# Second relative attention: the queries' write goes ahead of the relative values' read, and the queries' read three operations later on ScalarE

## The chip, the cores and the metric

The kernel runs on one core of a Trainium2 chip. The metric is the device time of one execution in microseconds (us). All numbers of one profiled execution are times from the start of its span.

## What is computed

`x` has 64 samples of 128 tokens with 128 features. Four layers add to it in turn: an attention over feature maps, a mixture of experts, an attention with relative positions, a second mixture of experts. The change lies in the third, which computes this (16 heads of 8 features, 77 keys a sample):

```
q = (query @ Wq + bq)                      # query = layernorm(x); k, v come from ctx
scores = einsum('bhqd,bhkd->bhqk', q, k)
rel_k = rel_key_table[ids]                 # ids = clip(q - k) + 128
scores = scores + einsum('bhqd,qkd->bhqk', q, rel_k)
attn = softmax(scores / sqrt(hd))
out = einsum('bhqk,bhkd->bhqd', attn, v)
out = out + einsum('bhqk,qkd->bhqd', attn, rel_value_table[ids])
x = x + tanh(g_xattn[1]) * (out @ Wo + bo)
```

## The kernel before, in words

`relative_attention` (from L1384) works one sample after the other. Each engine has its own program of slots: slot `n` does the scores of sample `n` and later stages of the samples before it. `slots` (L66) runs slots -4 to 67; the order of operations inside a slot is written out by hand for each engine, and engines meet at semaphores only. `p` is the parity of a sample and picks one of two buffers of nearly every tile; `o` is the other parity.

Two things of a sample make a detour through DRAM, because their rows have to be laid out anew over the partitions:

- The queries. TensorE projects them in slot `n-2` (`project`), ScalarE and VectorE write them as a high and a low float16 part (`high_parts` L1681, `low_parts` L1843, tile `a_q_parts`). SyncE writes them to DRAM (`write_queries`, L1485) once VectorE's part is there (`rows_low`). ScalarE's queue issues the read (`read_queries`, L1658) into `a_q_pos`, once the write has landed (`q_out`) and the scores of two samples before have been made. TensorE's `scores` need it (`q_in`).
- The relative part of the output. TensorE makes it in four quarters (`relative`, L1570), ScalarE copies each out of PSUM (`copy_relative`, L1715, tile `a_rel_all`). After the fourth copy SyncE issues eight writes (`write_relative`, L1492), and when all have landed (`r_out`) the read into `a_rel` (`read_relative`, L1498). GpSimd adds it to the mixed values (`add_relative`, L1777).

GpSimd's slot has three steps: `divide` (L1784), `mask_queries` (L1768, two instructions that spread the queries over the heads, tiles `a_q_head_high` and `a_q_head_low`), `add_relative`. In slot `n` the first is for sample `n-3`, the second for `n+1`, the third for `n-2`. TensorE's `scores(n, p, 0)`, the first step of its slot, waits for both instructions of `mask_queries(n)`.

ScalarE's slot before the change begins with these steps, and ends with `exp(n, 3)`:

```
read_queries(n + 1, o)
copy_rows(n - 2)
high_prob(n - 1, o, 2)
copy_relative(n - 1, o, 0)
high_prob(n - 1, o, 3)
```

`copy_rows` (L1722) takes the sums over the values out of PSUM, `high_prob` (L1703) the transposed probabilities. TensorE's `mix_turn` waits for the first, and its `relative(n-1, o, 1)` for `copy_relative(n-1, o, 0)`.

Of the kernel before, what the change touches and what calls it, by code (L numbers as in the profile page):

```python
# [53 lines left out]
def wait(eng, sem, value):  # L54

    if isinstance(value, int) and value <= 0:
        return
    eng.wait_ge(sem, value)  # L58


def inside(n, lo, hi):

    return lo <= n < hi if isinstance(n, int) else True


def slots(eng, first, lo, hi, last, body):  # L66

    for n in range(first, lo):
        body(n, n % 2)
    if hi > lo:  # L70
        with eng.Fori(0, (hi - lo) // 2) as i:
            for r in range(2):
                body(2 * i + (lo + r), (lo + r) % 2)
    for n in range(max(lo, hi), last):
        body(n, n % 2)
# [1308 lines left out]
def relative_attention(nc, B, io, x_all, stats, mean, rstd, xn_shift, ident, gates, ctx_t, tables, q_dram, r_dram):  # L1384
# [6 lines left out]
    with ExitStack() as ctx:  # L1391
# [80 lines left out]
        with nc.Block(name="a1") as block:  # L1472
            @block.sync
            def _(sp):
                for t, src in WEIGHTS:
                    sp.dma_start(t[:, :], io[src]).then_inc(weights_in, 16)
                sp.wait_ge(cleared, 1)
                for p in range(2):
                    sp.dma_start(q_read[p], q_pos[p][:, :, :]).then_inc(q_zeroed, 16)
                sp.wait_ge(q_zeroed, 32)  # L1480

                def write_queries(n, p):
                    if inside(n, 0, B):
                        sp.wait_ge(rows_low, n + 1)
                        sp.dma_start(q_written[p], q_parts[p][:, :, :].rearrange("q a (d h) -> q (a d) h", d=HD)  # L1485
                                     ).then_inc(q_out[p], 16)

                def write_relative(n, p):
                    if inside(n, 0, B):
                        sp.wait_ge(rel_copied, 4 * n + 4)  # L1490
                        for c in range(QC):
                            sp.dma_start(r_written[p][c], rel_all[p][c:P:QC, :, HD * c:HD * (c + 1)]  # L1492
                                         ).then_inc(r_out[p], 16)

                def read_relative(n, p):
                    if inside(n, 0, B):
                        sp.wait_ge(r_out[p], (n - p) * QC * 8 + QC * 16)
                        sp.dma_start(rel[p][:, :, :].rearrange("q h d -> q (h d)"), r_dram[p]).then_inc(r_in[p], 16)  # L1498

                def slot(n, p):  # L1500
                    read_relative(n - 2, p)
                    write_queries(n + 2, p)
                    write_relative(n - 1, 1 - p)

                slots(sp, FIRST, LO, HI, LAST, slot)

            @block.tensor
# [141 lines left out]
            def _(act):  # L1649
# [4 lines left out]
                def read_queries(n, p):  # L1654
                    if inside(n, 0, B):
                        act.wait_ge(q_out[p], (n - p) * 8 + 16)
                        wait(act, score_ready, 4 * n - 4)
                        act.dma_start(q_pos[p][:, :, :], q_read[p]).then_inc(q_in[p], 16)  # L1658
# [7 lines left out]
                def high_parts(n, p):  # L1666
                    o = 1 - p
                    if inside(n, -2, B):
                        act.wait_ge(proj_ready, n + 3)
                        if inside(n + 1, 0, B):  # L1670
                            wait(act, score_ready, 4 * n)
                            last = nc.scalar.activation(k_t[o][0][:, :], prep_ps[:, K_COLS], ACT.Identity,
                                                        bias=b_k[:, 0:1])
                        if inside(n, 0, B):
                            wait(act, mix_ready, n - 1)
                            last = nc.scalar.activation(value[p][:, :, 0:HD],
                                                        prep_ps[0:KC, V_COLS].rearrange("k (h d) -> k h d", d=HD),
                                                        ACT.Copy)
                        if inside(n + 2, 0, B):
                            wait(act, q_out[p], (n + 2 - p) * 8)  # L1680
                            nc.scalar.activation(q_parts[p][:, 0, :], prep_ps[:, ROW_COLS], ACT.Copy)  # L1681
                            wait(act, q_head_ready, 2 * n + 2)
                            last = nc.scalar.activation(q_t[p][0][:, :], prep_ps[:, Q_COLS], ACT.Identity,
                                                        bias=b_q[:, 0:1])
                        last.then_inc(proj_high, 1)

                def normalize(n, p):
                    if inside(n, 0, B):
                        wait(act, xn_t, n - 1)
                        nc.scalar.activation(xn[p][:, :], x_all[:, n, :], ACT.Identity, bias=xn_shift[:, n, :],  # L1690
                                             scale=rstd[:, n, :]).then_inc(xn_ready, 1)

                def exp(n, u):
                    if inside(n, 0, B):
                        act.wait_ge(shifted, 4 * n + u + 1)
                        nc.scalar.activation(prob[u][:, :, :], prob[u][:, :, :], ACT.Exp, scale=SCALE).then_inc(exped, 1)

                def high_prob(n, p, u):
                    if inside(n, 0, B):
                        act.wait_ge(prob_ready, 4 * n + u + 1)  # L1700
                        wait(act, rel_ready, 4 * n + u - 7)
                        wait(act, mix_ready, n - 1)
                        nc.scalar.activation(prob_t[p][0][:, 4 * u:4 * u + 4, :],  # L1703
                                             trans_ps[u % 2][0:KC, :].rearrange("k (g r) -> k g r", g=4),
                                             ACT.Copy).then_inc(prob_high, 1)

                def copy_relative(n, p, u):
                    if inside(n, 0, B):
                        act.wait_ge(rel_ready, 4 * n + u + 1)
                        if u == 0:  # L1710
                            wait(act, r_out[p], (n - p) * QC * 8)
                            wait(act, r_in[p], (n - p) * 8)
                        if u == 3:
                            wait(act, mixed_ready, n - 1)
                        nc.scalar.activation(rel_all[p][:, 4 * u:4 * u + 4, :].rearrange("r g w -> r (g w)"),  # L1715
                                             rel_ps[:, 0:4 * QC * HD], ACT.Copy).then_inc(rel_copied, 1)

                def copy_rows(n):
                    if inside(n, 0, B):
                        act.wait_ge(mix_ready, n + 1)  # L1720
                        wait(act, rows_turned, n)
                        nc.scalar.activation(mixed_rows[:, :, :].rearrange("r u q -> r (u q)"), rows_ps[:, :],  # L1722
                                             ACT.Copy).then_inc(rows_copied, 1)

                def high_mixed(n, p):
                    if inside(n, 0, B):
                        act.wait_ge(mixed_turned, n + 1)
                        wait(act, y_ready, n - 1)
                        nc.scalar.activation(mixed_t[p][0][:, :], fin_ps[:, 0:P], ACT.Copy).then_inc(mixed_high, 1)

                def slot(n, p):
                    o = 1 - p
                    read_queries(n + 1, o)
                    copy_rows(n - 2)
                    high_prob(n - 1, o, 2)
                    copy_relative(n - 1, o, 0)
                    high_prob(n - 1, o, 3)
                    high_parts(n, p)
                    copy_relative(n - 1, o, 1)
                    exp(n, 0)  # L1740
                    exp(n, 1)
                    copy_relative(n - 1, o, 2)
                    high_prob(n, p, 0)
                    normalize(n + 4, p)
                    high_mixed(n - 3, o)
                    exp(n, 2)
                    high_prob(n, p, 1)
                    copy_relative(n - 1, o, 3)
                    copy_xn(n + 3, o)
                    exp(n, 3)  # L1750

                slots(act, FIRST, LO, HI, LAST, slot)

            @block.gpsimd
# [315 lines left out]
```

## Time and profile before

| | us |
|---|---|
| median of 3 runs | 2211.84 (2209.42 to 2215.06) |
| the profiled execution | 2210.14, span 2208.4 |
| TensorE busy | 2051.3 (93%) |
| VectorE busy | 1913.1 (87%) |
| ScalarE busy | 1554.9 (70%) |
| GpSimd busy | 1575.4 (71%) |

Busy time is a sum over four layers with different limits, so these shares do not say what the changed stage is bound by. The second attention runs from about 1211 to 1800 us of the span. There the order of its slots and who waits for whom matter, read from the waits and from the timeline of each engine. The names ending in q (SPq, ACTq) are an engine's queue, which issues DMAs.

### The profile page before, as it was taken

The page shows a single profiled execution, that of the slowest core. Times are in us where ns is not written, and L with a number is a line of the kernel's source. Part 1 is how long each engine was busy: PE and PEld are TensorE (multiplying, and loading weights), DVE is VectorE, ACT ScalarE, POOL GpSimd, SP SyncE. Part 2 cuts the span into 40 slices and gives each one's busy share as a digit, 9 for nine tenths or more (in the row PEclk, how much of TensorE's full clock was granted, in tenths as well). Part 3 has the DMA queues.
Part 4 walks back from the last instruction along what each step waited for, and adds up shares of the span by engine and source line. Part 5 has one row for each costly group of instructions (what it writes and reads, how often), then busy time and mean ns, then how long its engine had stood idle before and what let it go on. Part 6 is the DMA issues. An engine that isn't in the chain of part 4 may idle for free. (4 is left out here: it accounts for less than half of the span.)

```text
span 2208.4 us, 82850 instructions
## 1 busy us (share of the span) xinstructions
PE 2051.3 (93%) x28378; PEld 1570.9 (71%) x28380; DVE 1913.1 (87%) x4327; ACT 1554.9 (70%) x3516; POOL 1575.4 (71%) x1457
## 2 busy tenths in 40 slices
PE   3999999977999999999996899999999966999999
PEld 2788888854666666666664889999999953666666
DVE  5899999987888888888887789999999868888888
ACT  3788888865555555555554677777777756888887
POOL 1567777643666666666665889999999943888887
PEclk9999999988999999999998899999999978999999
DMA  5000000004322222222221445555555520000000
GB/s 155 12 6 6 6 6 6 7 1 90 93 90 80 81 87 80 81 88 78 83 79 26 78 78 86 80 80 85 82 80 80 84 67 1 15 9 14 9 14 15
DMA packets 476443, 121.41 MB, mean 55 GB/s; under 512 B 431879, under 2 KB 446855, under 8 KB 475604
## 3 DMA queue, kind: packets, MB, share of 16 engines
q1 hardware_dynamic: 343988, 86.86, 18.2%
q10 hardware_dynamic: 132384, 33.63, 6.7%
q8 instruction: 42, 0.69, 0.1%
q14 instruction: 29, 0.24, 0.0%
HBM read 106.51 MB, written 13.89 MB: 55 GB/s over the span
## 5 line engine op out<-in xcount | busy, mean ns | idle before, releaser
L1220 POOL TENSOR_TENSOR f_low<-f_hidden,f_high 128x512 f16<-128x512 f32 x336 | 442.6, 1323 | 217.0 <-ACT f_high L1152 215.1
L1178 DVE TENSOR_TENSOR f_hidden<-f_hidden,f_share 128x512 f32<-128x512 f32 x336 | 374.1, 1114 | 0.0
L1367 POOL TENSOR_TENSOR f_low<-f_hidden,f_high 128x512 f16<-128x512 f32 x256 | 297.1, 1161 | 74.5 <-ACT f_high L1310 74.1
L1158 ACT ACTIVATE f_act_out<-f_gate 128x512 f32<-128x512 f32 x336 | 200.4, 597 | 192.4 <-PE f_gate L1122 192.4
L1201 DVE SCALAR_TENSOR_TENSOR f_hidden<-f_up,f_act_out 128x512 f32<-128x512 f32 x336 | 229.7, 684 | 83.6 <-PE f_up L1122 50.6
L1152 ACT ACTIVATE f_high<-f_hidden 128x512 f16<-128x512 f32 x336 | 210.5, 626 | 73.0 <-DVE f_hidden L1178 71.7
L1132 PE MATMUL f_y<-w_high,f_high 128*128 128x128 f16 x1344 | 242.4, 219 | 2.2 <-POOL f_low L1220 2.2
L1132 PE MATMUL f_y<-w_high,f_low 128*128 128x128 f16 x1344 | 242.4, 219 | 0.0
L1132 PE MATMUL f_y<-w_low,f_high 128*128 128x128 f16 x1344 | 242.4, 219 | 0.0
L1768 POOL TENSOR_TENSOR a_q_head_high<-a_q_t_high,a_head_mask 128x2048 f16<-128x2048 f16 x64 | 232.9, 3639 | 8.0 <-DVE a_q_t_low L1845 8.0
L1768 POOL TENSOR_TENSOR a_q_head_low<-a_q_t_low,a_head_mask 128x2048 f16<-128x2048 f16 x64 | 232.9, 3639 | 0.0
L1353 DVE SCALAR_TENSOR_TENSOR f_hidden<-f_in,f_act_out 128x512 f32<-128x512 f32 x256 | 175.6, 686 | 50.6 <-ACT f_act_out L1317 50.6
L1876 DVE TENSOR_TENSOR a_prob_t_low<-a_trans,a_prob_t_high 77x512 f16<-77x512 f32 x256 | 171.0, 669 | 39.6 <-ACT a_prob_t_high L1703 37.7
L1317 ACT ACTIVATE f_act_out<-f_in 128x512 f32<-128x512 f32 x256 | 152.9, 597 | 65.8 <-PE f_in L1279 60.3
L1548 PE MATMUL a_score<-a_k_t_high,a_q_head_high 128*128 128x77 f16 x1024 | 185.3, 203 | 9.6 <-POOL a_q_head_low L1768 6.4
L1291 PE MATMUL f_y<-w_high,f_high 128*128 128x128 f16 x1024 | 184.8, 219 | 1.8 <-DVE x_all L1331 0.6
L1548 PE MATMUL a_score<-a_k_t_low,a_q_head_high 128*128 128x77 f16 x1024 | 184.9, 203 | 0.0
L1550 PE MATMUL a_score<-table_high,a_q_pos 128*128 128x77 f16 x1024 | 184.8, 203 | 0.0
L1550 PE MATMUL a_score<-table_low,a_q_pos 128*128 128x77 f16 x1024 | 184.8, 203 | 0.0
L1548 PE MATMUL a_score<-a_k_t_high,a_q_head_low 128*128 128x77 f16 x1024 | 184.7, 202 | 0.0
L1291 PE MATMUL f_y<-w_high,f_low 128*128 128x128 f16 x1024 | 184.6, 219 | 0.0
L1291 PE MATMUL f_y<-w_low,f_high 128*128 128x128 f16 x1024 | 184.6, 219 | 0.0
(279 smaller groups left out, 8165.1 us busy)
## 6 DMA issues: line engine op xcount, KB each, us to landing
f_share<-expert_shares SPq DMA_DIRECT2D x128, 256.0 KB, 3.2
a_q_pos<-queries ACTq DMA_DIRECT2D x64, 512.0 KB, 4.4
f_share<-expert_shares SPq DMA_DIRECT2D x128, 128.0 KB, 3.0
relative_values<-a_rel_all SPq DMA_DIRECT2D x512, 8.0 KB, 2.5
x_all<-in_x SPq DMA_DIRECT2D x4, 1024.0 KB, 7.8
f_share<-expert_shares SPq DMA_DIRECT2D x128, 32.0 KB, 1.8
queries<-a_q_parts SPq DMA_DIRECT2D x64, 64.0 KB, 3.0
a_rel<-relative_values SPq DMA_DIRECT2D x64, 64.0 KB, 1.7
```

Source lines behind the costliest of these rows:

```text
L1132: mm = nc.tensor.matmul(dst, h[r][:, own], w_down[part][:, m, :], start=(m == 0 and t == 0 and k == 0), stop=(m == M - 1 and k == 2), skip ...
L1152: nc.scalar.activation(high[r][:, :], hidden[r][:, :], ACT.Copy).then_inc(high_ready, 1)
L1158: nc.scalar.activation(act_out[m % RING][:, :], gate_ps[m % BANKS][:, :], ACT.Silu, scale=1.0 / WSCALE).then_inc(act_ready, 1)
L1178: nc.vector.tensor_tensor(hidden[r][:, :], hidden[r][:, :], share[k][:, :, :].rearrange("p t q -> p (t q)"), ALU.mult).then_inc(scaled, 1)
L1201: nc.vector.scalar_tensor_tensor(out=hidden[r][:, :], in0=up_ps[m % BANKS][:, :], scalar=1.0 / WSCALE, in1=act_out[r][:, :], op0=ALU.mult, ...
L1220: nc.gpsimd.tensor_tensor(low[r][:, :], hidden[r][:, :], high[r][:, :], ALU.subtract).then_inc(low_ready, 1)
L1291: mm = nc.tensor.matmul(dst, h[m % RING][:, own], w_down[part][:, m, :], start=(c == 0 and t == 0 and k == 0), stop=(c == per - 1 and k == 2),
L1353: nc.vector.scalar_tensor_tensor(out=dst, in0=src, scalar=scalar, in1=a, op0=op, op1=ALU.mult).then_inc(hidden_ready, 1)
L1367: nc.gpsimd.tensor_tensor(low[k][:, :], hidden[k][:, :], high[k][:, :], ALU.subtract).then_inc(low_ready, 1)
L1548: nc.tensor.matmul(dst, q[:, QC * g:QC * (g + 1), :], t[:, :], start=(k == 0), stop=False)
L1550: mm = nc.tensor.matmul(dst, q_pos[p][:, g, :], key_table[k][:, 0, window], start=False, stop=(k == 1))
L1768: nc.gpsimd.tensor_tensor(q_head[p][k][:, :, :], q_t[p][k][:, :].unsqueeze(2).broadcast_to([P, P, NH]), head_mask[:, :].unsqueeze(1).broad ...
```

## The change

Two steps change places in two slots. On SyncE the write of the queries of sample `n+2` is issued before the read of the relative values of sample `n-2`. On ScalarE the read of the queries comes after `copy_rows`, `high_prob` and `copy_relative`. Nothing is added or removed.

```diff
@@ -1498,8 +1498,8 @@  (SyncE)
                 def slot(n, p):
+                    write_queries(n + 2, p)
                     read_relative(n - 2, p)
-                    write_queries(n + 2, p)
                     write_relative(n - 1, 1 - p)
@@ -1730,10 +1730,10 @@  (ScalarE)
                 def slot(n, p):
                     o = 1 - p
-                    read_queries(n + 1, o)
                     copy_rows(n - 2)
                     high_prob(n - 1, o, 2)
                     copy_relative(n - 1, o, 0)
+                    read_queries(n + 1, o)
                     high_prob(n - 1, o, 3)
                     high_parts(n, p)
                     copy_relative(n - 1, o, 1)
```

SyncE's queue in the middle slots, where two slots make one turn of the loop, before:

```order
L1498 DMA a_rel<-relative_values 128x128
L1484 REGISTER_ALU
L1485 DMA queries<-a_q_parts 128x16x16
L1490 ISA
L1492 DMA relative_values<-a_rel_all 16x16x8 x8
```

and after:

```order
L1485 DMA queries<-a_q_parts 128x16x16
L1497 ISA
L1498 DMA a_rel<-relative_values 128x128
L1490 ISA
L1492 DMA relative_values<-a_rel_all 16x16x8 x8
```

The write of the queries now stands behind the eight writes of the slot before, and the read of the relative values behind it.

ScalarE, from the last operation of one slot to `high_prob(n-1, o, 3)` of the next, before:

```order
L1696 ACTIVATE a_prob<-a_prob 128x308
L1656 REGISTER_ALU
L58 ISA
L1658 DMA a_q_pos<-queries 128x16x128
L1722 ACTIVATE a_mixed_rows<-a_rows 128x512
L58 REGISTER_ALU
L1703 ACTIVATE a_prob_t_high<-a_trans 77x512
L58 REGISTER_ALU
L1715 ACTIVATE a_rel_all<-a_rel 128x256
L58 REGISTER_ALU
L1703 ACTIVATE a_prob_t_high<-a_trans 77x512
```

and after:

```order
L1696 ACTIVATE a_prob<-a_prob 128x308
L1722 ACTIVATE a_mixed_rows<-a_rows 128x512
L58 REGISTER_ALU
L1703 ACTIVATE a_prob_t_high<-a_trans 77x512
L58 REGISTER_ALU
L1715 ACTIVATE a_rel_all<-a_rel 128x256
L1656 REGISTER_ALU
L58 ISA
L1658 DMA a_q_pos<-queries 128x16x128
L58 REGISTER_ALU
L1703 ACTIVATE a_prob_t_high<-a_trans 77x512
```

The DMA and its two waits (L1656, L58) moved behind three ACTIVATEs.

## Rows read from the trace of the kernel before

**Rows 1.** Busy time by stretch: second attention, and its middle; columns in the first line.

```profile
core 0: us, PE busy (x) PEld busy (x) DVE busy (x) ACT busy (x) POOL busy (x), PEclk, DMA share, GB/s
1211.00:1800.00 589.00, 560.55 (x12719) 521.07 (x12719) 509.95 (x1399) 431.72 (x1274) 515.11 (x254) 0.98 0.50 79
1340.00:1740.00 400.00, 391.94 (x9020) 365.44 (x9017) 362.11 (x999) 305.11 (x907) 366.21 (x182) 1.00 0.52 82
```

**Rows 2.** Waits, 1340 to 1740 us: engine, what, releaser: us in total, times, longest.

```profile
ACT a_mixed_rows L1722 <- DMA queries<-a_q_parts: 69.5, 46, 1.9
POOL a_mixed L1777 <- DMA a_rel<-relative_values: 30.3, 45, 1.0
...
PEld a_rel L1570 <- issue: 8.3, 32, 0.4
...
PE a_score L1548 <- POOL a_q_head_low L1768: 3.5, 11, 0.4
```

**Rows 3.** GpSimd's instructions of line L1768, 1340 to 1740 us.

```profile
L1768 POOL TENSOR_TENSOR a_q_head_high<-a_q_t_high,a_head_mask x46: 3635/3640/3645, 1340.0 to 1736.6; 128x2048 f16<-128x2048 f16 x46
```

**Rows 4.** Timeline of GpSimd: start, us, instruction, [idle before and releaser].

```profile
1607.98 3.64 POOL L1768 TENSOR_TENSOR a_q_head_low<-a_q_t_low,a_head_mask 128x2048 f16<-128x2048 f16 x1
1612.23 0.46 POOL L1777 TENSOR_TENSOR a_mixed<-a_mixed,a_rel 128x128 f32<-128x128 f32 x1 [0.61 <-DMA a_rel<-relative_values]
1612.77 0.41 POOL L1784 TENSOR_TENSOR a_mixed<-a_mixed,a_rden 128x128 f32<-128x128 f32 x1
1613.13 3.64 POOL L1768 TENSOR_TENSOR a_q_head_high<-a_q_t_high,a_head_mask 128x2048 f16<-128x2048 f16 x1
1616.73 3.64 POOL L1768 TENSOR_TENSOR a_q_head_low<-a_q_t_low,a_head_mask 128x2048 f16<-128x2048 f16 x1
1621.01 0.46 POOL L1777 TENSOR_TENSOR a_mixed<-a_mixed,a_rel 128x128 f32<-128x128 f32 x1 [0.63 <-DMA a_rel<-relative_values]
```

**Rows 5.** Timeline of TensorE around the first scores of slots, and in one slot.

```profile
1603.04 0.21 PE L1548 MATMUL a_score<-a_k_t_high,a_q_head_high 128*128 128x77 f16 x1
...
1611.95 0.21 PE L1548 MATMUL a_score<-a_k_t_high,a_q_head_high 128*128 128x77 f16 x1 [0.29 <-POOL a_q_head_low L1768]
...
1613.35 0.64 PE L1559 MATMUL a_trans<-a_by_head_ident,a_prob 128*77 128x128 f32 x4
...
1614.37 0.19 PE L1570 MATMUL a_rel<-table_high,a_prob_t_low 77*128 77x64 f16 x1
...
1620.51 0.21 PE L1548 MATMUL a_score<-a_k_t_high,a_q_head_high 128*128 128x77 f16 x1
...
1629.47 0.21 PE L1548 MATMUL a_score<-a_k_t_high,a_q_head_high 128*128 128x77 f16 x1 [0.27 <-POOL a_q_head_low L1768]
```

**Rows 6.** Timeline of SyncE's queue, two slots (a write of eight counts as one row).

```profile
1603.90 5.10 SPq L1492 DMA_DIRECT2D relative_values<-a_rel_all  x8
...
1612.48 5.11 SPq L1492 DMA_DIRECT2D relative_values<-a_rel_all  x8
1619.17 0.34 SPq L1498 DMA_DIRECT2D a_rel<-relative_values  x1
1619.62 0.37 SPq L1485 DMA_DIRECT2D queries<-a_q_parts  x1
```

**Rows 7.** Timeline of ScalarE and its queue over the start of two slots.

```profile
1605.19 0.38 ACTq L1658 DMA_DIRECT2D a_q_pos<-queries  x1
...
1612.08 0.38 ACT L1715 ACTIVATE a_rel_all<-a_rel 128x256 f32<-128x256 f32 x1
...
1613.93 0.39 ACTq L1658 DMA_DIRECT2D a_q_pos<-queries  x1
1614.51 0.60 ACT L1722 ACTIVATE a_mixed_rows<-a_rows 128x512 f32<-128x512 f32 x1 [1.54 <-DMA queries<-a_q_parts]
1615.00 0.58 ACT L1703 ACTIVATE a_prob_t_high<-a_trans 77x512 f16<-77x512 f32 x1
1615.48 0.38 ACT L1715 ACTIVATE a_rel_all<-a_rel 128x256 f32<-128x256 f32 x1
1615.75 0.60 ACT L1703 ACTIVATE a_prob_t_high<-a_trans 77x512 f16<-77x512 f32 x1
```

**Rows 8.** Landing of the fourth of the eight writes issued from 1612.48.

```profile
L1492 SPq DMA_DIRECT2D relative_values<-a_rel_all x1: 612/612/612, 1614.4 to 1614.4; - x1
...
DMA to landing us min/median/max: 3.9/3.9/3.9
```

**Rows 9.** Landing of the first of the eight, and of the eighth.

```profile
L1492 SPq DMA_DIRECT2D relative_values<-a_rel_all x1: 538/538/538, 1612.5 to 1612.5; - x1
...
DMA to landing us min/median/max: 1.9/1.9/1.9
...
L1492 SPq DMA_DIRECT2D relative_values<-a_rel_all x1: 609/609/609, 1617.0 to 1617.0; - x1
...
DMA to landing us min/median/max: 2.2/2.2/2.2
```

**Rows 10.** An early slot: queues of SyncE and ScalarE, GpSimd, landing of the eighth write.

```profile
1294.31 5.11 SPq L1492 DMA_DIRECT2D relative_values<-a_rel_all  x8
1301.61 0.34 SPq L1498 DMA_DIRECT2D a_rel<-relative_values  x1
...
1296.89 0.39 ACTq L1658 DMA_DIRECT2D a_q_pos<-queries  x1
...
1303.45 0.46 POOL L1777 TENSOR_TENSOR a_mixed<-a_mixed,a_rel 128x128 f32<-128x128 f32 x1 [1.55 <-DMA a_rel<-relative_values]
...
DMA to landing us min/median/max: 2.8/2.8/2.8
```

**Rows 11.** VectorE's low part of the queries; DMA issues: KB each, median us to landing.

```profile
1617.75 0.28 DVE L1843 TENSOR_TENSOR a_q_parts<-a_prep,a_q_parts 128x128 f16<-128x128 f32 x1
...
a_q_pos<-queries ACTq DMA_DIRECT2D x64, 512.0 KB, 4.4
...
queries<-a_q_parts SPq DMA_DIRECT2D x64, 64.0 KB, 3.0
a_rel<-relative_values SPq DMA_DIRECT2D x64, 64.0 KB, 1.7
```

## The prediction

> **What bounds the kernel now.** The busy times by stretch come first. In the middle of the second attention TensorE is busy for 391.94 of 400 us, GpSimd for 366.21 and VectorE for 362.11 [rows 1]. That looks like a stage bound by TensorE, but a share says nothing about who sets the pace, so the waits come next. The largest is ScalarE's: 69.5 us in 46 slots before its copy of the mixed rows, 1.5 us a slot, released by the landing of the queries' write [rows 2]. This is the wait that the change goes for. The second is GpSimd's for the relative values, 30.3 us in 45 slots, 0.67 each. TensorE waits for GpSimd's `a_q_head_low` in only 11 [rows 2].
>
> The small waits lead to the pace. GpSimd masks 46 samples between 1340.0 and 1736.6 us [rows 3], so a slot is 396.6 / 45 = 8.81 us. Its own work in one is two masks of 3.64, an add of 0.46 and a divide of 0.41, about 8.15; the rest is its wait for the relative read [rows 4]. Its masks end at 1611.62 and 1620.37 (start plus 3.64, rows 4), and TensorE's first scores of the slots start 0.33 and 0.14 later [rows 5]. So TensorE enters both slots on GpSimd's release, even where the modelled end of its last matmul hides the gap.
>
> Hence the loop, followed over three slots: scores start at 1603.04 [rows 5]; the fourth copy of the relative part ends on ScalarE at 1612.46 (1612.08 plus 0.38, rows 7); SyncE issues its first write at 1612.48, and the read at 1619.17 [rows 6]; GpSimd adds at 1621.01 [rows 4], then has a divide and two masks to do, and scores start at 1629.47 [rows 5]. That is 9.42 + 8.55 + 8.46 = 26.43 us for three slots, 8.81 each: exactly the slot length. **A delay d in this loop costs d / 3 per slot, and a gain in it gives as little.** ScalarE's wait of 1.5 us is not one of its links: it falls at the start of a slot, and TensorE's work lies between it and the fourth copy.
>
> **The change, part by part.** *SyncE.* The queries' write was issued after the relative read, at 1619.62 [rows 6]. It now needs SyncE free (1612.48 + 5.11 = 1617.59, rows 6) and VectorE's low part (1617.75 + 0.28 = 1618.03, rows 11), so it goes out at about 1618.1, 1.5 us earlier. Its 0.37 us of issue end before 1619.17, when the relative read could start, so the read is not held on SyncE: cost nothing, as long as the eight writes land no sooner than that; with that cover gone SyncE would owe the read up to 0.45 us (wait for VectorE) plus 0.37. The write lands 3.0 us after issue [rows 11], at 1621.1, well before its reader needs it.
>
> *ScalarE's wait* goes: from 1.5 us to nothing. What is late next is TensorE. Its transposes start at 1613.35 for 0.64 us and the relative quarter's last matmul at 1614.37 for 0.19 [rows 5]. So ScalarE's `high_prob` can start at about 1614.15, and `copy_relative` 0.48 later (as 1615.00 to 1615.48, rows 7), at 1614.64 instead of 1615.48. The queries' read follows at about 1615.0, 1.1 us later than now (1613.93). ScalarE needs 0.58 from that issue to its next operation (1613.93 to 1614.51, rows 7), so `high_prob(n-1, o, 3)` starts near 1615.6 instead of 1615.75. Of 1.5 us of wait only 0.15 are left there. The gain inside the loop is TensorE's: it stands before `relative` L1570 for 8.3 us in 45 slots [rows 2], 0.18 us each, mostly for the copy that now comes 0.8 us earlier. I take 0.18 as gained. The landing of the queries, 4.4 us after issue [rows 11], moves to 1619.4; scores need it at 1620.51 [rows 5]. Covered by 1.1 us; without that cover each microsecond would be paid in full.
>
> *What the later read collides with.* The eight writes of the relative part are issued over 5.1 us from 1612.48, the queries' read (512 KB) at 1613.93 in their midst. The first write lands after 1.9 us, the fourth, issued 0.5 us behind the read, after 3.9, the eighth after 2.2 [rows 8, 9]: the read holds up the writes issued behind it, and they have just about caught up by the eighth. Only the eighth counts, since the relative read waits for all. With the read at 1615.0, 2.5 us after the first write, the hold falls on the last three or four. One early slot shows this timing: writes from 1294.31, the queries' read at 1296.89, 2.58 us behind. There the eighth landed after 2.8 instead of 2.2 us, the relative read went out 7.30 us after the first write instead of 6.69, and GpSimd's add came 9.14 after it instead of 8.53 [rows 4, 6, 10]. The slot from 1603.90 with its read 1.29 behind had 8.33 [rows 4, 6, 7]. So three points: 1.29, 1.45 and 2.58 us behind give 8.33, 8.53 and 9.14. From the mean of the first two, 8.43, to 2.5 behind I read +0.65, nearest to the third row. Ends: 0 if the writes escape, about +1.95 if the queries' write, which takes 3.0 - 1.7 = 1.3 us longer to land than the relative read [rows 11] and now is ahead of it in the same queue, is waited for in full. I take nothing for the latter: the write goes out a microsecond ahead of the read.
>
> The Trainium skill's page "DMA: Bandwidth & Descriptors", section "Queues, rings and completion order", says that each DMA engine takes turns between the queues it has work for, packet by packet. By that rule the writes would slip in between the packets of the queries' read, the hold would be nothing, and the sum -3.6 instead of +9.4 us. The trace does not agree: 3.9 us for the fourth write.
>
> *Sum.* Per loop of three slots +0.65 - 0.18 = +0.47, per slot +0.157, over some 60 of 64 slots (the first and last run on other waits) +9.4 us. On the profiled execution's 2210.1 us that is 2219.5; the median of the runs lies 1.7 us above it, so 2221.
>
> **The rivals.** *Nothing moves* (22%). The writes' delay is absorbed or does not occur, and the 0.18 us of TensorE are all that comes: -0.18 / 3 x 60 = -3.6, about 2208. For it: the eighth write was issued 2 us behind the late read. Against: the slot from 1294.31 [rows 10]. By the rule of the skill named above this is the outcome.
>
> *Faster* (8%). The later read lets most writes through before it starts, and the tail that still reaches the eighth now (2.2 us against 1.9 for the first, rows 9) is gone: -0.3 - 0.18 per loop, -9.6 us, 2202. It decides if the read's hold starts only after the eighth write is on its way, which needs the read some 4 us behind the first write rather than 2.5. ScalarE would have to reach it much later than its rows allow.
>
> *Much slower* (15%). The relative read also queues behind the queries' write. If a third of the 1.3 us shows, d grows by 0.45: (0.65 + 0.45 - 0.18) / 3 x 60 = +18, 2230; in full +35, 2247. It decides where the write's transfer is not over when the read is issued; for it speaks that held writes push that transfer later, against it that the read is pushed as far.
>
> *TensorE was the bound after all.* Then GpSimd's lateness costs less than a third of d per slot, since its 0.67 us of wait are slack. It gives 2208 to 2214 and is counted with the first rival. Against it stand 0.33 and 0.14 us between masks and scores in both parities.
>
> **How the numbers follow.** My forecast has 55%, and by itself runs from 2215 (d = 0.4) to 2227 (d = 1.0). A measurement of this kernel tells about 0.3% from no change, 6.6 us: slower begins at 2218.5. Slower: four fifths and more of the 55% and the 15%, some 0.61. Same: the 22% and the forecast's low end, less a little that could be faster, 0.30. Faster 0.09. The range, 2206 to 2232, takes in the first rival and the lower part of the much slower one, and leaves out the faster one and the worst.
>
> **What would show it.** Right: ScalarE's wait for `queries<-a_q_parts` gone from the waits; queries' read about 3.1 us after the first scores of a slot and 2.5 after the first of the eight writes; the eighth write landing after 2.7 to 3 us; GpSimd's wait before L1777 risen from 0.67 to above 0.8 a slot; slots of 8.95 us or more. Wrong: the eighth write still at 2.2 us; GpSimd's wait unchanged; or slots that lengthen while masks end well before the scores start, which would mean a wait for `a_q_pos`.

## The result, and the profile after

The changed kernel takes 2233.97 us (median of 4 runs, 2230.78 to 2236.23) against 2212.32 us for the kernel before on the same chip (4 runs, 2209.42 to 2215.06): ratio 1.0097, 95% interval 1.0079 to 1.0115. It is slower by 21.7 us, where 9 were forecast, and it lies 2 us above the range. Its profiled execution took 2233.33 us, with a span of 2231.5.

Nearly all of the loss is in the second attention: from the first start of GpSimd's masks to the last it takes 582.6 us (1215.3 to 1797.9) instead of 561.5 (1211.3 to 1772.8), 21.1 of the 23.1 us by which the two profiled spans differ. The busy times of the middle 400 us of the changed kernel, answering to [rows 1], and the first and last mask there, answering to [rows 3]:

```profile
1340.00:1740.00 400.00, 371.25 (x8638) 351.80 (x8634) 350.04 (x958) 301.10 (x869) 350.14 (x174) 1.00 0.50 79
```

```profile
L1768 POOL TENSOR_TENSOR a_q_head_high<-a_q_t_high,a_head_mask x44: 3636/3642/3646, 1336.4 to 1732.6; 128x2048 f16<-128x2048 f16 x44
```

Every engine does less in the same time, TensorE too (371 us instead of 392), and a slot takes 396.2 / 43 = 9.21 us instead of 8.81. The waits of the changed kernel over the same stretch, to be read against [rows 2]:

```profile
ACT a_prob_t_high L1703 <- PE a_trans L1559: 57.0, 88, 2.8
POOL a_mixed L1777 <- DMA a_rel<-relative_values: 46.3, 42, 2.8
PEld a_score L1548 <- issue: 32.7, 40, 1.9
PE a_score L1548 <- POOL a_q_head_low L1768: 27.8, 37, 1.8
```

ScalarE's wait for the queries' write, 69.5 us before, is gone. Its wait for TensorE's transposes rose instead, from 10.2 to 57.0 us. GpSimd's wait for the relative values rose from 30.3 us in 45 slots to 46.3 in 42, from 0.67 to 1.10 each. TensorE's wait for GpSimd's masks, 3.5 us in 11 slots before, is now 27.8 in 37: it enters its slots on GpSimd's release.

One slot of the changed kernel shows how. First SyncE's queue, to be read against [rows 6]:

```profile
1500.80 5.11 SPq L1492 DMA_DIRECT2D relative_values<-a_rel_all  x8
1506.65 0.37 SPq L1485 DMA_DIRECT2D queries<-a_q_parts  x1
1508.77 0.33 SPq L1498 DMA_DIRECT2D a_rel<-relative_values  x1
```

Then ScalarE and its queue, against [rows 7]:

```profile
1501.16 0.60 ACT L1722 ACTIVATE a_mixed_rows<-a_rows 128x512 f32<-128x512 f32 x1
1502.77 0.59 ACT L1703 ACTIVATE a_prob_t_high<-a_trans 77x512 f16<-77x512 f32 x1 [1.00 <-PE a_trans L1559]
1503.35 0.38 ACT L1715 ACTIVATE a_rel_all<-a_rel 128x256 f32<-128x256 f32 x1
1503.62 0.39 ACTq L1658 DMA_DIRECT2D a_q_pos<-queries  x1
```

GpSimd, against [rows 4]:

```profile
1505.82 3.64 POOL L1768 TENSOR_TENSOR a_q_head_low<-a_q_t_low,a_head_mask 128x2048 f16<-128x2048 f16 x1
1510.63 0.46 POOL L1777 TENSOR_TENSOR a_mixed<-a_mixed,a_rel 128x128 f32<-128x128 f32 x1 [1.17 <-DMA a_rel<-relative_values]
```

And the landing of the eighth write, issued at 1505.3, against [rows 9]:

```profile
L1492 SPq DMA_DIRECT2D relative_values<-a_rel_all x1: 609/609/609, 1505.3 to 1505.3; - x1
...
DMA to landing us min/median/max: 3.5/3.5/3.5
```

The queries' read goes out 2.82 us behind the first write, the eighth write lands after 3.5 us instead of 2.2, the relative read goes out 7.97 us behind the first write instead of 6.69, and the add comes after 9.83 instead of 8.53.

### The profile page after: what moved, and what is told of

Its sections match the earlier page's. It is cut to its first block and busy times, and to the rows that moved or that the text cites. A ratio compares the mean times of both kernels' runs of the same rounds, so it can differ in the third digit from the quotient of the medians.

```text
span 2231.5 us, 82852 instructions
## 1 busy us (share of the span) xinstructions
PE 2051.4 (92%) x28380; PEld 1578.7 (71%) x28380; DVE 1917.8 (86%) x4327; ACT 1566.3 (70%) x3516; POOL 1573.6 (71%) x1457
## 5 line engine op out<-in xcount | busy, mean ns | idle before, releaser
L1768 POOL TENSOR_TENSOR a_q_head_high<-a_q_t_high,a_head_mask 128x2048 f16<-128x2048 f16 x64 | 233.1, 3641 | 8.0 <-DVE a_q_t_low L1845 8.0
L1768 POOL TENSOR_TENSOR a_q_head_low<-a_q_t_low,a_head_mask 128x2048 f16<-128x2048 f16 x64 | 232.9, 3640 | 0.0
L1703 ACT ACTIVATE a_prob_t_high<-a_trans 77x512 f16<-77x512 f32 x256 | 151.0, 590 | 111.9 <-PE a_trans L1559 87.7
```

The costliest lines, as they stand in the source:

```text
L1768: nc.gpsimd.tensor_tensor(q_head[p][k][:, :, :], q_t[p][k][:, :].unsqueeze(2).broadcast_to([P, P, NH]), head_mask[:, :].unsqueeze(1).broad ...
```

## The experiments

Four numbers are compared throughout. They are means over the slots of samples 14 to 55, each taken from the timelines as in the slot above: **slot** is the time from the first scores of one sample to those of the next; **read Q**, **read R** and **add** are the issue of the queries' read, the issue of the relative read and GpSimd's add, all counted from the issue of the first of the eight writes. **R to add** is the difference of the last two. The ratio is against the kernel before on the same chip. The experiments ran on four other chips, where that one takes 2216 to 2217 us, 4 to 5 more than on the first, so times are compared only through ratios. It was profiled on the first chip and on one of the others, the changed kernel on the same two. The two profiles of one kernel differ by up to 0.07 us in the slot and up to 0.18 in the other columns, so smaller differences between rows are not resolved. A ratio of 0.9992 for the kernel before against itself shows what a ratio can be off.

| | ratio (95%) | slot | read Q | read R | R to add | add |
|---|---|---|---|---|---|---|
| before, first chip | 1 | 8.81 | 1.46 | 6.70 | 1.84 | 8.54 |
| before again | 0.9992 (0.9982 to 1.0002) | 8.88 | 1.54 | 6.84 | 1.88 | 8.72 |
| changed, first chip | 1.0097 (1.0079 to 1.0115) | 9.22 | 2.86 | 7.83 | 1.98 | 9.82 |
| changed again | 1.0086 (1.0068 to 1.0104) | 9.24 | 2.87 | 8.01 | 1.92 | 9.93 |
| SyncE's exchange alone | 1.0013 (1.0004 to 1.0022) | 8.95 | 0.00 | 6.55 | 2.60 | 9.16 |
| ScalarE's move alone | 1.0044 (1.0031 to 1.0057) | 9.11 | 2.76 | 7.67 | 1.94 | 9.61 |
| exchange, read after 1 operation | 1.0019 (1.0008 to 1.0029) | 8.95 | 0.01 | 6.56 | 2.59 | 9.14 |
| exchange, read after 2 operations | 1.0036 (1.0021 to 1.0052) | 9.04 | 2.07 | 7.27 | 2.08 | 9.36 |
| exchange, half a queries' write | 0.9941 (0.9918 to 0.9963) | 8.74 | -0.28 | 6.49 | 1.97 | 8.46 |
| two writes on ScalarE | 1.0066 (1.0052 to 1.0081) | 9.28 | 1.84 | 6.66 | 1.90 | 8.55 |
| one write on ScalarE, read late | 1.0020 (1.0010 to 1.0030) | 9.03 | 2.67 | 7.48 | 1.89 | 9.38 |
| two writes, read late | 0.9985 (0.9975 to 0.9994) | 8.92 | 2.58 | 7.16 | 1.89 | 9.05 |
| two writes, read behind high_prob | 1.0001 (0.9991 to 1.0012) | 9.05 | 3.16 | 7.51 | 1.91 | 9.42 |
| two writes, read behind high_parts | **0.9963** (0.9949 to 0.9976) | 8.83 | 3.58 | 5.31 | 3.12 | 8.44 |

**Each half alone.** The kernel before with one of the two hunks of the diff.

```diff
 SyncE alone
-                    read_relative(n - 2, p)
                     write_queries(n + 2, p)
+                    read_relative(n - 2, p)
 ScalarE alone
-                    read_queries(n + 1, o)
                     copy_rows(n - 2)
                     high_prob(n - 1, o, 2)
                     copy_relative(n - 1, o, 0)
+                    read_queries(n + 1, o)
```

> Only SyncE's two steps are exchanged; ScalarE still issues the queries' read first in its slot. Theory A (two causes: the later read of the queries holds the last writes of the relative part, and the queries' write directly behind the eighth write delays its landing): ScalarE's wait for the queries' write nearly gone, the queries' read about 0.5 us behind the first of the eight writes instead of 1.4; the relative read 6.8 to 7.1 us behind the first write (before 6.7, changed kernel 7.8); time 2208 to 2219. Rival R1 (all of the loss is the later queries' read): 6.5 us or less and 2203 to 2210. Rival R2 (all of the loss is the queries' write ahead of the relative read): 7.8 us and about 2233.

> Only ScalarE's step is moved; SyncE keeps read before write. Theory A: the eighth write is held by the queries' read but nothing follows it, so the relative read goes out 7.3 to 7.5 us behind the first write; slots of 8.95 to 9.05 us, time 2219 to 2226. R1: 7.8 us and about 2233. R2: 6.7 us and 2206 to 2210.

Both halves cost, neither costs all: 1.0013 and 1.0044. That rules out both rivals with a single cause. They do not add up either: the move alone costs 0.44%, both together 0.86 to 0.97%, so with the move in place the exchange costs another 0.42 to 0.53%. With ScalarE's move alone the relative read goes out at 7.67, later than the 7.3 to 7.5 expected, and slots take 9.11 instead of 8.95 to 9.05; only the ratio is where theory A has it. With the exchange alone the relative read is even earlier than before (6.55, not 6.8 to 7.1), since the queries' read is now issued at the same time as the first write and the writes have long caught up by the eighth, which lands 1.94 us after its issue (mean of the slots whose landing the trace has). But the add comes 2.60 us behind the relative read instead of 1.84. Theory A had put the cost of the exchange on the eighth write's landing, and that was wrong; the late part is the relative read itself. Its row in the kernel with the exchange alone (x44, 1340 to 1740 us), whose landing was 1.6/1.7/1.9 in the same stretch of the kernel before:

```profile
L1498 SPq DMA_DIRECT2D a_rel<-relative_values x44: 337/550/832, 1345.9 to 1731.3; - x44
...
DMA to landing us min/median/max: 2.2/2.6/2.8
```

One slot of that kernel, SyncE's queue and GpSimd:

```profile
1506.56 0.36 SPq L1485 DMA_DIRECT2D queries<-a_q_parts  x1
1507.35 0.57 SPq L1498 DMA_DIRECT2D a_rel<-relative_values  x1
...
1509.99 0.46 POOL L1777 TENSOR_TENSOR a_mixed<-a_mixed,a_rel 128x128 f32<-128x128 f32 x1 [0.86 <-DMA a_rel<-relative_values]
```

The read is issued 0.79 us behind the queries' write (over the slots 0.5 to 1.2), and the add follows 2.64 later.

**Half a queries' write.** Is it that write's packets that the relative read stands behind? The exchange alone, with half of the write left out (the low part of the queries, which the scores' position term then lacks).

```diff
-                        sp.dma_start(q_written[p], q_parts[p][:, :, :].rearrange("q a (d h) -> q (a d) h", d=HD)
+                        sp.dma_start(q_written[p][:, 0:HD, :], q_parts[p][:, 0, :].rearrange("q (d h) -> q d h", d=HD)
```

> SyncE's exchange alone, and the queries' write leaves out the low part of the queries (half of its packets; the scores then lack the low part in their position term). In the kernel with the exchange alone GpSimd's add came 2.6 us behind the issue of the relative read, where the kernel before has 1.84. If that is the relative read queueing behind the packets of the queries' write: 1.9 to 2.1 us here, slots as short as those of the kernel before or shorter, ratio 0.996 to 1.000. If the read is slow for another reason: 2.4 to 2.7 us and the ratio of the exchange alone, 1.001.

R to add falls from 2.60 to 1.97, the slot from 8.95 to 8.74 us and the ratio to 0.9941, below the range that was expected. So the read does queue behind the queries' write. The ratio is not that of a usable kernel. It is better than the kernel before because half of the transfer is gone; how much of that belongs to the order cannot be told, since the kernel before was not run with half a write.

**Where the queries' read stands.** SyncE's exchange as in the change, the read one or two operations later instead of three.

```diff
                     copy_rows(n - 2)
+                    read_queries(n + 1, o)
                     high_prob(n - 1, o, 2)
                     copy_relative(n - 1, o, 0)
-                    read_queries(n + 1, o)
```

The other version has it between `high_prob` and `copy_relative`.

> SyncE's exchange as in the change, the queries' read one operation later (after copy_rows) instead of three. Theory A: the read is issued 0.4 to 1.0 us behind the first of the eight writes; the writes have caught up by the eighth; relative read 6.5 to 6.7 us behind the first write, and it queues behind the queries' write (add 2.3 to 2.7 us behind the read's issue); ratio 1.001 to 1.004. If the place of the read on ScalarE does not matter: as the changed kernel, 1.0097.

> The same with the queries' read two operations later (after high_prob). Theory A: the read is issued 2.0 to 2.6 us behind the first write, three or four writes are held, relative read 7.2 to 7.7 us behind the first write, ratio 1.005 to 1.009, between the kernel with the read one operation later and the changed kernel.

Behind `copy_rows` the read is issued no later than in front of it (0.01 against 0.00, where 0.4 to 1.0 was expected; the relative read, the add and the ratio are in their ranges). ScalarE's queue does not wait for the operation in front of the DMA: the read goes out 0.36 us before `copy_rows` has even started (mean over the slots, 0.22 to 0.48). Behind `high_prob`, which waits for TensorE, it comes at 2.07, the relative read at 7.27, and the ratio 1.0036 misses the expected 1.005 to 1.009 on the low side. With eight writes on SyncE the last of which is issued 4.5 us behind the first, read Q and read R now make one series: 0.00 and 6.55, 1.46 and 6.70, 2.07 and 7.27, 2.76 and 7.67, 2.86 and 7.83. Flat at first, then about 0.8 us for 1 us: from 1.46 to 2.86 it is 1.13 / 1.40 = 0.81, and between the two profiles of the other chip (1.54 and 6.84, 2.87 and 8.01) 1.17 / 1.33 = 0.88.

**The same chip for both.** The kernel before and the changed kernel, unedited.

> The kernel before, unchanged, profiled on the chip of these runs, so that slots are compared on one chip. All theories: ratio 1, slots of 8.8 to 8.9 us, relative read 6.7 us behind the first of the eight writes, add 8.5 behind it.

> The changed kernel, unchanged, on the same chip. All theories: ratio near 1.0097, slots about 0.4 us longer than those of the kernel before, relative read 7.8 us and add 9.8 us behind the first write.

They repeat the first chip's picture: slots 0.36 us apart instead of 0.41.

**Getting the writes out of the way.** If SyncE's eight issues are the link, ScalarE can issue two of them where it waits anyway.

```diff
-                        for c in range(QC):
+                        for c in range(QC - 2):
                             sp.dma_start(r_written[p][c], rel_all[p][c:P:QC, :, HD * c:HD * (c + 1)]
                                          ).then_inc(r_out[p], 16)
+                def write_rest(n, p):
+                    if inside(n, 0, B):
+                        act.wait_ge(rel_copied, 4 * n + 4)
+                        for c in range(QC - 2, QC):
+                            act.dma_start(r_written[p][c], rel_all[p][c:P:QC, :, HD * c:HD * (c + 1)]
+                                          ).then_inc(r_out[p], 16)
...
                     exp(n, 3)
+                    write_rest(n - 1, o)
```

> The kernel before, but of the eight writes of the relative part ScalarE's queue issues the last two, after exp(n, 3), where it waits 1.5 us anyway. If SyncE's eight issues (5.1 us) are a link of the loop of three slots, it shortens by up to 1.2 us, until TensorE's own work (about 8.45 us a slot) is the bound: slots of 8.45 to 8.6 us, time 2188 to 2200. If TensorE or something else was the bound before: within 2208 to 2214.

This one missed badly: 1.0066. SyncE's last issue came at 3.25 us instead of 4.54, and the relative read did not move (6.66). Fewer issues are worth nothing while the queries' read stands in front of the last writes. ScalarE, besides, was late: the two issues took about 1.5 us of its queue, the queries' read and `copy_rows` came behind them, and the fourth copy of the relative part ended 10.1 us after the first scores instead of 9.5. Here TensorE waited for `copy_rows` in each slot, which the kernel before did not do in its first profile and did for 0.5 us in two slots of the second:

```profile
ACT a_mixed_rows L1729 <- issue: 85.4, 43, 2.2
...
PEld a_mix L1596 <- ACT a_mixed_rows L1729: 18.2, 43, 0.5
```

Next the queries' read was moved as well, with two writes and with one on ScalarE, SyncE in its old order (the diff is the one above, with `QC - 1` for one write, plus the ScalarE half of the change).

> ScalarE issues the last two of the eight writes after exp(n, 3), and the queries' read three operations later as in the change; SyncE keeps its old order with six writes. Theory A: the queries' read is issued about 3.3 us behind the first write, that is behind all eight writes, and holds none; the relative read goes out 5.2 to 5.7 us behind the first write (before 6.7), TensorE becomes the bound at 8.45 to 8.6 us a slot, ratio 0.988 to 0.995. If the read still gets ahead of the sixth write: 6.5 us or more and ratio 1.00 to 1.01. Rival (the hold is no matter, the moved read costs by coming late): ratio above 1.005.

> The same with one write on ScalarE and seven on SyncE. Theory A: the queries' read is issued about 3 us behind the first write, ahead of SyncE's sixth and seventh, which are held: relative read 7.0 to 7.5 us behind the first write, ratio 1.000 to 1.006, clearly slower than with two writes moved.

With two writes the read was issued at 2.58, not 3.3: here too the queue did not wait for the operation in front, and the read went out 0.56 us before that one ended. SyncE's sixth write (3.36) was still behind it. 7.16 is what was expected for that case, and 0.9985 just under its 1.00 to 1.01; beside the 0.9992 of the unedited kernel it is no clear gain. With one write it is 7.48 and 1.0020, as expected. Two more places for the read decide it, each one step further down ScalarE's slot, behind `high_prob(n-1, o, 3)` or behind `high_parts(n, p)` as here (against the version with two writes just described):

```diff
                     copy_relative(n - 1, o, 0)
-                    read_queries(n + 1, o)
                     high_prob(n - 1, o, 3)
                     high_parts(n, p)
+                    read_queries(n + 1, o)
```

> Two writes on ScalarE, SyncE's old order, and the queries' read behind one more operation (high_prob(n-1, o, 3)). In the version with the read three operations later it was issued 2.6 us behind the first write, ahead of SyncE's last one (3.4), and the relative read still went out 7.2 us behind the first write. Theory A (what counts is whether the queries' read is issued ahead of the last write): the read moves to 2.9 to 3.3 us behind the first write, close to the last write; the relative read at 5.5 to 7.2, ratio 0.990 to 0.999. Rival (the eight writes land late with two queues issuing, wherever the read stands): 7.0 to 7.3 and 0.9985.

> The same with the queries' read behind high_parts(n, p) as well. Theory A: the read is issued 3.6 to 4.2 us behind the first write, behind all eight; the relative read goes out 5.2 to 5.7 us behind the first write. The loop of three slots is then no longer the bound; the queries land about 4.4 us after issue, that is 8.3 to 8.7 us after the first scores of the slot before, so slots are 8.5 to 8.75 us by TensorE's work or by that landing, ratio 0.986 to 0.996. Rival: relative read at 7.0 us or more, ratio 0.998 or above.

At 3.16 the read is still ahead of the last write (3.49), and the relative read goes out at 7.51, later than both theory A (5.5 to 7.2) and the rival (7.0 to 7.3) had it. At 3.58 it is behind the last one (3.21), and the relative read goes out at 5.31, as theory A had it. A step of 0.4 us in the one moves the other by 2.2 us.

The single slots of these two kernels show where the step lies. Two neighbouring slots of the last version, with the read behind `high_parts`; in each the sixth write on SyncE's queue is the last 0.61 us of the row of six:

```profile
1506.04 3.82 SPq L1492 DMA_DIRECT2D relative_values<-a_rel_all  x6
1509.57 0.37 ACTq L1658 DMA_DIRECT2D a_q_pos<-queries  x1
1511.30 0.34 SPq L1498 DMA_DIRECT2D a_rel<-relative_values  x1
...
1514.86 3.81 SPq L1492 DMA_DIRECT2D relative_values<-a_rel_all  x6
1518.22 0.39 ACTq L1658 DMA_DIRECT2D a_q_pos<-queries  x1
1521.91 0.34 SPq L1498 DMA_DIRECT2D a_rel<-relative_values  x1
```

In the first the queries' read goes out 0.32 us behind the issue of the sixth write and the relative read 5.26 us behind the first write. In the second it goes out 0.16 us behind it, the sixth write lands after 3.8 us, and the relative read goes out 7.05 us behind the first write. Of the 42 slots, the 40 with 0.19 us or more between the two have the relative read at 5.15 to 5.37, the two with 0.14 and 0.16 at 7.06. The other version has three slots in which the read goes out behind the last write, by 0.07 to 0.18 us, and they are held as well (6.98 to 7.46). So it is the order of issue that decides, and not the number of writes or their queue, but a write that went out less than about 0.2 us ahead of the read is held too. The kernel before shows the same, mostly at its third write: in the same slots, the 17 writes issued up to 0.19 us ahead of the read landed after 3.4 to 3.9 us, and 21 of the 22 issued 0.20 to 0.37 us ahead after 2.1 to 2.4.

The last version is the fastest real one, 0.9963, just outside the 0.986 to 0.996 expected. In it the hold has moved to the relative read, which now is behind the queries' read, though on the other queue; one slot, the two queues and then GpSimd:

```profile
1612.11 3.81 SPq L1492 DMA_DIRECT2D relative_values<-a_rel_all  x6
1617.28 0.34 SPq L1498 DMA_DIRECT2D a_rel<-relative_values  x1
...
1615.76 0.37 ACTq L1658 DMA_DIRECT2D a_q_pos<-queries  x1
...
1620.33 0.46 POOL L1785 TENSOR_TENSOR a_mixed<-a_mixed,a_rel 128x128 f32<-128x128 f32 x1 [0.58 <-DMA a_rel<-relative_values]
```

Its relative read lands after 1.7/3.1/3.4 us (minimum, median, maximum; the low end is the two held slots), and TensorE waits for the queries, 7.5 us in 27 slots, which it does in no other kernel here:

```profile
PE a_score L1548 <- DMA a_q_pos<-queries: 7.5, 27, 0.5
```

So slots were 8.83 us and not 8.5 to 8.75, against 8.81 and 8.88 in the two profiles of the kernel before, neither of them from this chip: the gain in the middle is not resolved. From the first mask to the last it takes 559.5 us (1213.3 to 1772.8), the kernel before 561.5 and 565.5 (1210.9 to 1776.4). Of the 6.0 us against the second profile, 2.4 are in the middle slots and 3.6 outside them.

## Why the prediction was right and wrong

**What bounds the stage: right.** The loop over three slots, through the eight writes, the relative read, the add and the masks, carried the loss of the middle slots, 16.8 us of the 21.1. Its arithmetic closes: the add moved from 8.54 to 9.82 us behind the first write, +1.28; the way from a slot's first scores to the fourth copy became 0.12 shorter (9.49 to 9.37); a third of the difference is 0.39 us a slot, and 0.41 were measured. Over 60 slots that is 23 to 25 us, for 21.7 measured. On the other chip it closes too: (1.21 - 0.21) / 3 = 0.33, and 0.36 measured.

**The gain on ScalarE: right in kind.** The wait of 1.5 us went away and nearly nothing came of it. 0.18 us were forecast for the loop; 0.12 came on the first chip and 0.21 on the other.

**The step that failed is d, the term "+0.65".** It measured +1.28 (+1.21 on the other chip), and with it the forecast's own sum gives (1.28 - 0.18) / 3 x 60 = 22 us, where 21.7 were measured. That the sum comes so near is in part luck: it gives every slot the same price, and the slots outside the middle lost about half as much each (4.3 us in 22 slots against 16.8 in 41). Three things are in it, two about the later read and one about the exchange, which had been put at nothing:

- *The queries' read at "2.5 us behind the first write".* It went out at 2.86. Against the first scores of its slot it went out at 3.04, where the forecast had it (3.1). It is the writes that came nearer to it. The read is tied to the first scores of its slot, the eight writes to those of the slot before. When slots lengthen by 0.4 us, the read falls that much further behind the writes and holds them longer: the loss feeds itself. In the kernel before the first write came 0.71 us behind the first scores of the slot whose queries' read disturbs it, in the changed kernel 0.19 us (means over the same slots). I worked the offset out for slots of 8.81 us and did not go round the loop again with the new length.
- *The price of an offset.* I read it from three single slots, among them an early one with 7.30 us at 2.58. The series of means gives 0.81 us for each 1 us, so 7.6 there. With ScalarE's move alone, where no queries' write is in the way, most of the 1.28 is already there: 7.67 instead of 6.70 for the relative read, 9.61 instead of 8.54 for the add (8.72 on the other chip, so 0.9 to 1.1). The early slot was a poor stand-in because slots scatter: of the changed kernel's slots, the 11 with the read 2.4 to 2.8 us behind have the relative read at 7.38 to 8.17, mean 7.71, and 7.30 lies below them all.
- *"I take nothing for the latter", and "cost nothing" for the exchange.* In the middle slots it is the small part of d: 9.82 instead of 9.61. In the time it is about half of the loss, 0.42 to 0.53% of 0.86 to 0.97%. From the first scores of the first sample to those of the last the move alone takes 575.5 us, the changed kernel 582.7 and 586.1, the kernel before 561.5 and 565.5. Part of the exchange's cost lies outside the middle, which the sum priced like the rest: the first 14 and last 8 slots take 203.5 to 207.4 us in the four kernels with the whole queries' write issued first and eight writes on SyncE, 200.4 to 201.8 in the kernel before and with the move alone. What it does there was not traced further.

**How the exchange acts in the middle slots.** Alone, the exchange makes the relative read queue behind the queries' write for 0.76 us, the mechanism of the rival *much slower*, which I had priced at a third of 1.3 us. In the changed kernel the relative read goes out 1.9 us behind that write, with the exchange alone 0.9 (means), and R to add is 1.98, near the 1.84 of the kernel before. Against ScalarE's move alone (9.61) the changed kernel has 9.82: the exchange adds 0.21 to the add, 0.16 of it before the relative read is issued. Whether that part is the eighth write landing later with the queries' write directly behind it is open. The eighth write lands 3.09 us after its issue with the move alone and 3.23 in the changed kernel, but the read is also 0.10 us later there, worth 0.08 by the series, and the two profiles of the changed kernel differ by 0.18 in read R. A version in which the queries' write waits for the eight landings has no measured time.

**The rule of the Trainium skill** that DMA engines take turns between queues ("DMA: Bandwidth & Descriptors", "Queues, rings and completion order") does not describe what counts here. Small writes issued on SyncE's queue after the large read on ScalarE's land up to 2 us late, and the step from 3.16 to 3.58 shows that being issued first is what spares them. The packet records of the kernel before show two phases in each slot: around the read's first packets SyncE's queue starts none for 1.2 to 1.6 us, and after that packets of both queues start side by side. The forecast was right to go by the row of 3.9 us.

**The rivals.** "Nothing moves" and "TensorE was the bound" fell: TensorE's busy share dropped with the rest. "Much slower" had the nearest time (2230 to 2247), but not for its reason: the wait behind the queries' write is 0.14 of the 1.28 us (R to add, 1.84 to 1.98). Two ends in the working are off by 1 us and change nothing: with the 1.7 us added as in the sum, d = 0.4 and d = 1.0 give 2216 and 2228. "Faster" named its condition correctly, a read behind the last write; with two writes moved to ScalarE that condition was met, and the kernel was faster (0.9963).

## What to carry to other kernels

A wait on an engine with time to spare, like ScalarE's 1.5 us here, may be worth nothing to remove by itself; ask which transfers start or finish elsewhere because of the move. Issue a large DMA (here 512 KB) behind the last of the small DMAs that a loop waits for, with some tenths of a us between them, or so early that they catch up, and not into their midst; here that held across the queues of two engines. Price an offset from many slots and not from one that happens to show it. Where the moved step is tied to the slot and the work it disturbs to the slot before, recompute the offset with the longer slot until it stops changing.

## What the runs showed of the hardware

- Of eight small writes on SyncE's queue, those issued behind a 512 KB read on ScalarE's queue landed after up to 3.9 us instead of 1.9 [rows 8, 9], and in the changed kernel the eighth after 3.5 instead of 2.2 (means over the slots 3.23 and 2.14). The step is sharp: in the kernel before, the writes issued up to 0.19 us ahead of the read were held like those behind it (3.4 to 3.9 us), those issued 0.20 to 0.37 us ahead were not, but for one (2.1 to 2.4).
- The same in the other direction: the relative read, 64 KB on SyncE's queue, landed after 3.1 us (median) instead of 1.7 when issued 1.3 to 2.0 us behind ScalarE's 512 KB read, and after 2.6 when issued 0.5 to 1.2 us behind a 64 KB write on its own queue; with half of that write left out the add followed after 1.97 us instead of 2.60.
- ScalarE's queue issues a DMA before the operation in front of it has finished, or even started: behind `copy_rows` it went out at the same moment as in front of it, 0.36 us before `copy_rows` began; in the changed kernel 0.16 us before the end of `copy_relative`.
